# A graph network's second feed-forward matmul split into three float32r terms, with the splitting shared among VectorE and GpSimd

## What is computed

```python
# layer 0
attn_out = attn_out @ Wo + bo
h1 = _layer_norm(x + attn_out, g1, be1)
ff = jax.nn.relu(h1 @ W1 + b1) @ W2 + b2        # W1 512x1024, W2 1024x512
return _layer_norm(h1 + ff, g2, be2)
...
# layer 1
edge_feat = jnp.concatenate([x[src], x[dst], edge_attr], axis=-1)
h = mish(edge_feat @ W1 + b1)
messages = mish(h @ W2 + b2)
agg = jax.ops.segment_sum(messages, dst, num_segments=x.shape[0])
...
x = _layernorm(x + _L0_gnn_ref(...), axis=-1)
x = _layernorm(x + _L1_gnn_ref(...), axis=-1)
```

## Time and profile before

| | before |
|---|---|
| median of three runs | 244.72 us |
| the profiled execution | 245.73 us |
| its span, first to last instruction | 243.8 us |
| PE busy | 230.8 us, 95% |
| DVE busy | 153.4 us, 63% |
| ACT busy | 120.6 us, 49% |
| POOL busy | 6.8 us, 3% |
| granted TensorE clock, mean | 0.990 |
| DMA moved | 25.48 MB |

### The profile page before, as it was taken

One profiled execution on the slowest core, in us unless ns is written; L12 is line 12 of the kernel. 1 busy time (PEld: TensorE's weight loads), 2 busy tenths in 40 slices (PEclk: granted clock), 3 DMA queues, 4 the chain that ended last, 5 costly groups with the idle time before them and its releaser, 6 DMA issues.

```text
span 243.8 us, 3226 instructions
## 1 busy us (share of the span) xinstructions
PE 230.8 (95%) x1231; PEld 185.9 (76%) x1231; DVE 153.4 (63%) x271; ACT 120.6 (49%) x220; POOL 6.8 (3%) x18
## 2 busy tenths in 40 slices
PE   7999999998999999999999999999999999997980
PEld 3977788765676787888888888888888889996760
DVE  3639785577579655875856848758558454363625
ACT  0326198747729834745735646457355343244000
POOL 0020000001000000000000000000000000000001
PEclk9999999999999999999999999999999999999995
DMA  6999979930690000009022050040000000000001
GB/s 208 307 400 386 397 249 383 356 137 0 163 255 15 0 0 0 3 8 330 5 100 76 0 172 1 9 166 0 0 0 3 0 0 0 3 0 0 3 0 44
DMA packets 12320, 25.48 MB, mean 105 GB/s; under 512 B 1017, under 2 KB 1937, under 8 KB 11921
## 3 DMA queue, kind: packets, MB, share of 16 engines
q1 hardware_dynamic: 11520, 24.78, 30.0%
q10 hardware_dynamic: 784, 0.50, 0.8%
HBM read 25.01 MB, written 0.26 MB: 104 GB/s over the span
## 4 chain that ended last, share of the span: by engine, by line
PE 86%; DVE 6%; ACT 3%; issue 2%; POOL 1%; POOLq 0%; DVEq 0%; ACTq 0%
PE bank L668 36%; PE bank L651 12%; PE bank L463 9%; PE bank L472 6%; PE bank L519 4%; PE bank L535 3%; PE bank L678 3%; PE bank L679 3%; PE bank L482 2%; PE bank L446 1%; ACT WsT L408 1%; PE bank L630 1%; DVE y L884 1%; PE bank L631 1%; PE bank L635 1%
## 5 line engine op out<-in xcount | busy, mean ns | idle before, releaser
L668 PE MATMUL bank<-W2hi,Hhi 128*128 128x512 f32 x128 | 49.8, 389 | 0.0
L668 PE MATMUL bank<-W2hi,Clo 128*128 128x512 f32 x128 | 49.8, 389 | 0.0
L668 PE MATMUL bank<-W2lo,Hhi 128*128 128x512 f32 x128 | 49.8, 389 | 0.0
L380 ACT ACTIVATE Mhi<-M 128x512 fp32r<-128x512 f32 x32 | 20.2, 632 | 45.4 <-DVE M L994 45.4
L999 DVE TENSOR_TENSOR Mlo<-M,Mhi 128x512 fp32r<-128x512 f32 x32 | 22.1, 690 | 24.4 <-ACT M L381 24.4
L994 DVE TENSOR_TENSOR M<-bank,b2r 128x512 f32<-128x512 f32 x32 | 22.0, 687 | 12.6 <-PE bank L679 7.6
L668 PEld LDWEIGHTS bank<-W2hi,Clo 128*128 128x128 f32 x128 | 24.0, 188 | 5.0
L668 PEld LDWEIGHTS bank<-W2hi,Hhi 128*128 128x128 f32 x128 | 24.0, 188 | 5.0
L668 PEld LDWEIGHTS bank<-W2lo,Hhi 128*128 128x128 f32 x128 | 24.0, 188 | 5.0
L373 ACT ACTIVATE Hhi<-C 128x512 fp32r<-128x512 f32 x32 | 20.0, 625 | 12.4 <-DVE C L980 12.1
L293 ACT ACTIVATE C<-bank,cols 128x512 f32<-128x512 f32 x32 | 19.9, 685 | 11.6 <-PE bank L519 11.5
(11 more groups left out here) (193 smaller groups left out, 314.6 us busy)
## 6 DMA issues: line engine op xcount, KB each, us to landing
F<-in_L_gnn_W SPq DMA_DIRECT2D x2, 2048.0 KB, 14.3
W1raw<-in_L_gnn_W SPq DMA_DIRECT2D x1, 2048.0 KB, 22.5
ids<-in_src SPq DMA_DIRECT2D x2, 1024.0 KB, 14.0
W<-in_L_gnn_W SPq DMA_DIRECT2D x1, 2048.0 KB, 8.6
Wq<-in_L_gnn_Wq SPq DMA_DIRECT2D x4, 256.0 KB, 4.5
Wk<-in_L_gnn_Wk SPq DMA_DIRECT2D x4, 256.0 KB, 7.0
Wv<-in_L_gnn_Wv SPq DMA_DIRECT2D x1, 1024.0 KB, 10.1
ea<-in_edge_attr SPq DMA_DIRECT2D x1, 1024.0 KB, 11.8
```

The costliest lines, as they stand in the source:

```text
L380: act.activation(Mhi[:, t, :], M[:, t, :], ACT.Mish)
L668: done = mm(ST2[t][:, :], x[:, c, e], w[:, c, :], start=c == 0 and i == 0, stop=c == KC - 1 and i == 2)
```

## The change

It makes the second feed-forward of three float32r terms. ffT is rounded to `ffThi` by DVE and its remainder `ffTlo` made by POOL; F2 is rounded to `F2hi` by DVE, in the place of F1: the chunk pair i goes to the columns that group i of the first feed-forward has used, so it waits for `f1_done`. POOL makes `F2lo`. PE then does 48 float32r matmuls instead of 16 float32 ones, with the same edge steps between. F2 is loaded in W1raw's place of the queue and the reverse; W2raw's place is now used by ffThi, and its load waits for `f2_done` = 2. ACT makes W1hi behind the relus, among its edge steps. W1's remainders are shared: chunks 0 to 3 by POOL behind the feed-forward's, 4 and 5 by DVE behind the one-hots, 6 and 7 by DVE around the casts of xs.

```diff
-                        ("F2", 24, 8, F32), ("MA", 48, 4, F32), ("W2raw", 52, 4, F32), ("attn", 56, 2, F32), ("Wo", 60, 4, F32),
-                        ("W1raw", 64, 8, F32), ("EAThi", 72, 4, F32R), ("Wchi", 76, 1, F32R), ("Wc", 77, 1, F32), ("ffT", 78, 2, F32),
+                        ("W1raw", 24, 8, F32), ("MA", 48, 4, F32), ("W2raw", 52, 4, F32), ("attn", 56, 2, F32), ("Wo", 60, 4, F32),
+                        ("F2", 64, 8, F32), ("EAThi", 72, 4, F32R), ("Wchi", 76, 1, F32R), ("Wc", 77, 1, F32), ("ffT", 78, 2, F32),
...
+        split = overlay(("F2hi", 16, 8, F32R), ("W1lo", 24, 8, F32R), ("ffThi", 52, 2, F32R), ("xhi", 78, 1, F32R), ("xlo", 79, 1, F32R))
...
+        F2hi = split["F2hi"].rearrange("p (a h i n) -> p i a h n", a=2, h=2, i=FC // 2)
...
-            sp.dma_start(W1raw, w_view(a["L1_gnn_W1"][0:2 * D, :])).then_inc(S["w1_in"], 16)
+            sp.dma_start(F2, w_view(a["L0_gnn_W2"])).then_inc(S["f2_in"], 16)
...
-            sp.dma_start(F2, w_view(a["L0_gnn_W2"])).then_inc(S["f2_in"], 16)
+            sp.dma_start(W1raw, w_view(a["L1_gnn_W1"][0:2 * D, :])).then_inc(S["w1_in"], 16)
...
+            sp.wait_ge(S["f2_done"], 2)
             sp.dma_start(W2raw, w_view(a["L1_gnn_W2"])).then_inc(S["w2_in"], 16)
...
+            inverse_deviation(1)
+
+            for i in range(FC // 2):
+                for k in (2 * i, 2 * i + 1):
+                    pool.wait_ge(S["f2_hi"], k + 1)
+                    pool.tensor_tensor(F2lo[:, k, :].rearrange("p (h n) -> p h n", h=2), F2[:, k, :].rearrange("p (h n) -> p h n", h=2),
+                                       F2hi[:, i, k % 2].bitcast(F32), ALU.subtract).then_inc(S["f2_lo"], 1)
+                pool.wait_ge(S["ff_hi"], i + 1)
+                two = slice(2 * i, 2 * i + 2)
+                pool.tensor_tensor(ffTlo[:, two, :], ffT[:, two, :], ffThi[:, two, :].bitcast(F32), ALU.subtract).then_inc(S["ff_lo"], 1)
+            for c in range(KC):
+                pool.wait_ge(S["w1_hi"], c // 2 + 1)
+                pool.tensor_tensor(W1lo[:, c, :], W1raw[:, c, :], W1hi[:, c, :].bitcast(F32), ALU.subtract).then_inc(S["w1_lo_dst"], 1)
+            for n in range(1, 8):
+                inverse_deviation(n + 1)
...
-            act.wait_ge(S["w1_in"], 16)
             for i in range(4):
-                w1_high(i)
                 relu_out(i)
                 if i >= 1:
                     edge_term_out(range(i - 1, i))
             features_high(3)
-            edge_term_out(range(3, RING_STEPS))
+            act.wait_ge(S["w1_in"], 16)
+            for i in range(4):
+                w1_high(i)
+                edge_term_out(range(i + 3, i + 4))
+            edge_term_out(range(7, RING_STEPS))
...
-                columns_by((bank[1], bank[2]), ffT, F2, h, range(0, 3), 0, FC - 1)
+            def second_feed_forward(h, ks):
+
+                for k in ks:
+                    pe.wait_ge(S["f2_hi"], k + 1)
+                    pe.wait_ge(S["ff_hi"], k // 2 + 1)
+                    part = slice(D // 2 * h, D // 2 * (h + 1))
+                    whole = (bank[1], bank[2])[h][:, 0:D // 2]
+                    mm(whole, ffThi[:, k, :], F2hi[:, k // 2, k % 2, h, :], start=k == 0, stop=False)
+                    pe.wait_ge(S["f2_lo"], k + 1)
+                    mm(whole, ffThi[:, k, :], F2lo[:, k, part], start=False, stop=False)
+                    pe.wait_ge(S["ff_lo"], k // 2 + 1)
+                    done = mm(whole, ffTlo[:, k, :], F2hi[:, k // 2, k % 2, h, :], start=False, stop=k == FC - 1)
+                return done
...
-            for c in range(2 * KC):
-                dve.wait_ge(S["w1_hi"], c // 2 + 1)
-                v.tensor_tensor(W1lo[:, c, :], W1raw[:, c, :], W1hi[:, c, :].bitcast(F32), ALU.subtract).then_inc(S["w1_lo"], 1)
+            dve.wait_ge(S["f2_in"], 16)
+            for i in range(FC // 2):
+                dve.wait_ge(S["f1_done"], i + 1)
+                for k in (2 * i, 2 * i + 1):
+                    v.tensor_copy(F2hi[:, i, k % 2], F2[:, k, :].rearrange("p (h n) -> p h n", h=2)).then_inc(S["f2_hi"], 1)
+                dve.wait_ge(S["ff_ready"], 2 * (i + 1))
+                two = slice(2 * i, 2 * i + 2)
+                v.tensor_copy(ffThi[:, two, :], ffT[:, two, :]).then_inc(S["ff_hi"], 1)
...
             source_onehots(1)
+            w1_low((4, 5))
...
             norm(y[:, :], xs[:, :], S["nx_ready"])
+            w1_low((6,))
...
+            w1_low((7,))
             out_halves(xT_flat, xs_banks, S["nT_done"], 2, S["nT_ready"])
```

More of the change, by code:

```diff
@@ L96, in gnn_kernel @@
         first = overlay(("Wq", 0, 4, F32), ("Wk", 4, 4, F32), ("Wv", 8, 4, F32), ("ea", 12, 4, F32), ("F1", 16, 8, F32),
-                        ("F2", 24, 8, F32), ("MA", 48, 4, F32), ("W2raw", 52, 4, F32), ("attn", 56, 2, F32), ("Wo", 60, 4, F32),
-                        ("W1raw", 64, 8, F32), ("EAThi", 72, 4, F32R), ("Wchi", 76, 1, F32R), ("Wc", 77, 1, F32), ("ffT", 78, 2, F32),
+                        ("W1raw", 24, 8, F32), ("MA", 48, 4, F32), ("W2raw", 52, 4, F32), ("attn", 56, 2, F32), ("Wo", 60, 4, F32),
+                        ("F2", 64, 8, F32), ("EAThi", 72, 4, F32R), ("Wchi", 76, 1, F32R), ("Wc", 77, 1, F32), ("ffT", 78, 2, F32),
                         ("rows", 80, 7, F32), ("EATlo", 91, 4, F32R))
-        other = overlay(("Dbf", 28, 4, BF16), ("Sbf", 52, 4, BF16), ("W1hi", 56, 8, F32R), ("W1lo", 64, 8, F32R),
-                        ("ids0", 48, 4, I32), ("ids1", 87, 4, I32), ("Wclo", 77, 1, F32R), ("xhi", 78, 1, F32R), ("xlo", 79, 1, F32R))
+        other = overlay(("Dbf", 28, 4, BF16), ("Sbf", 52, 4, BF16), ("W1hi", 56, 8, F32R), ("F2lo", 64, 8, F32R), ("ffTlo", 78, 2, F32R),
+                        ("ids0", 48, 4, I32), ("ids1", 87, 4, I32), ("Wclo", 77, 1, F32R))
+        split = overlay(("F2hi", 16, 8, F32R), ("W1lo", 24, 8, F32R), ("ffThi", 52, 2, F32R), ("xhi", 78, 1, F32R), ("xlo", 79, 1, F32R))
         low = overlay(("Clo", 0, 32, F32R), ("Mlo", 64, 4, F32R))
@@ L119, in gnn_kernel @@
         Dbf, Sbf = chunks(other["Dbf"], ET), chunks(other["Sbf"], ET)
-        W1hi, W1lo = chunks(other["W1hi"], 2 * KC), chunks(other["W1lo"], 2 * KC)
-        xhi, xlo = chunks(other["xhi"], KC), chunks(other["xlo"], KC)
+        W1hi, W1lo = chunks(other["W1hi"], 2 * KC), chunks(split["W1lo"], 2 * KC)
+        xhi, xlo = chunks(split["xhi"], KC), chunks(split["xlo"], KC)
+        ffThi, ffTlo, F2lo = chunks(split["ffThi"], FC), chunks(other["ffTlo"], FC), chunks(other["F2lo"], FC)
+        F2hi = split["F2hi"].rearrange("p (a h i n) -> p i a h n", a=2, h=2, i=FC // 2)
         C = edge["C"].rearrange("p (g j e) -> p g j e", g=G, j=KC)
@@ L276, in _, with inverse_deviation @@
             inverse_root(1, small[:, 1:2], small[:, 2:3], S["deg_ready"], S["dinv_ready"])
-            for n in range(8):
-                inverse_root(n + 1, mv[:, 1:2], rstd[:, :], S["stat_ready"], S["rstd_ready"])
+            def inverse_deviation(n):
+                inverse_root(n, mv[:, 1:2], rstd[:, :], S["stat_ready"], S["rstd_ready"])
+            inverse_deviation(1)
[12 more added lines that the diff above has]
+                inverse_deviation(n + 1)
         @block.scalar
@@ L605, in _ @@
             turn_features(3)
-            pe.wait_ge(S["f2_in"], 16)
+            def second_feed_forward(h, ks):
[10 more added lines that the diff above has]
+                return done
             for h in range(2):
-                columns_by((bank[1], bank[2]), ffT, F2, h, range(0, 3), 0, FC - 1)
+                second_feed_forward(h, range(0, 3))
                 edge_term(range(2 * h + 3, 2 * h + 4))
-                columns_by((bank[1], bank[2]), ffT, F2, h, range(3, FC - 2), 0, FC - 1)
+                second_feed_forward(h, range(3, 6))
                 edge_term(range(2 * h + 4, 2 * h + 5))
-                if h == 0:
-                    pe.wait_ge(S["ff_ready"], FC)
-                columns_by((bank[1], bank[2]), ffT, F2, h, range(FC - 2, FC), 0, FC - 1).then_inc(S["f2_done"], 1)
+                second_feed_forward(h, range(6, FC)).then_inc(S["f2_done"], 1)
                 if h == 0:
@@ L624, in _ @@
             pe.wait_ge(S["w1_hi"], 4)
-            pe.wait_ge(S["w1_lo"], 8)
+            pe.wait_ge(S["w1_lo_dst"], KC)
             for b, c0 in ((bank[1], 0), (bank[2], KC)):
@@ L636, in _ @@
                 done.then_inc(S["ab_done"], 1)
+                if c0 == 0:
+                    pe.wait_ge(S["w1_lo"], KC)
             pe.wait_ge(S["nT_ready"], 4)
@@ L928, in _, with w1_low @@
             features_low(2)
-            for c in range(2 * KC):
-                dve.wait_ge(S["w1_hi"], c // 2 + 1)
-                v.tensor_tensor(W1lo[:, c, :], W1raw[:, c, :], W1hi[:, c, :].bitcast(F32), ALU.subtract).then_inc(S["w1_lo"], 1)
+            dve.wait_ge(S["f2_in"], 16)
[6 more added lines that the diff above has]
+                v.tensor_copy(ffThi[:, two, :], ffT[:, two, :]).then_inc(S["ff_hi"], 1)
             features_low(3)
+            def w1_low(cs):
```

(3 more changed lines are left out.)

4 lines of the change are left out of this document (2 added, 2 removed).

## The result

| us | before | after |
|---|---|---|
| time, median | 245.2 (244.4 to 246.1, 4 runs) | 253.4 (253.2 to 253.8, 4 runs) |
| span of the profiled execution | 243.8 | 251.7 |
| its mean granted clock of PE | 0.990 | 0.975 |

The change makes the kernel slower by 3.4%, a ratio of 1.034 [1.032, 1.036], or 8.2 us. The prediction had the sign and too little of the size: 2.3 us, with 249.8 as its upper end.

What follows compares the result with a forecast made beforehand. It took the chain as PE's up to 56.69, then DVE's normalisation. Terms +1.1, +1.2, +1.2 and -0.55 made +3.0, or +1.6 with shorter POOL slots; the middle, +2.3, gave 248.0 from 245.73, median 247.0, range 244.8 to 249.8.

Steps and rivals of the forecast that it cites:

- PE's matmuls: Second feed-forward on PE: 48 float32r matmuls at 0.12 us replace 16 float32 ones, saving 1.3 us in all.
- POOL, right in the sum: POOL's feed-forward subtractions: 1.26 us each, 0.70 for half size, plus 1.5 for casts between; last piece at 51.2.
- The casts, held: DVE's casts from SBUF between POOL's subtractions: 0.15 us each, between 0 and 0.3; ten make 1.5 us.
- The prediction's sum by the pages, 249.2: Whole kernel if DVE and POOL block one another in full, a cast at 0.3 us: 249.2 us.
- DVE starts the graph copies at 52.2: DVE behind PE's graph transposes: copies start at 52.2 where they were at 51.09, +1.1 us.
- The step that failed: DVE's one-hots beside POOL: taken as single rate, 0.66 to 0.71 us for 512 elements, and not held.
- The first is held until 56.2: +1.2: First of DVE's two new W1 subtractions, behind the one-hots: held by POOL's W1 subtractions until 56.2, +1.2 us.
- The new subtractions +1.2 and the residual -0.55: DVE before the statistics: two W1 subtractions at 0.60 us add 1.2; the residual no longer waits for PE, -0.55.
- What was costed at nothing: W1lo(6) ahead of xhi's casts, W1lo(7) and xT, ACT's W1hi, W2hi's later load, exchanged F2 and W1raw loads: no cost.
- Rival 3, the clock: PE's clock falls in a 3 us pause before the transposes of xs: 2.3 to 3.5 us more, 249.9; chance 0.12.
- Rivals 1 and 2: DVE beside POOL: first, nothing held, 244.9 us, chance 0.22; second, only two-input instructions held, 245.6 us, chance 0.14.
- the prediction's upper one: Delay at DVE's statistics with POOL's slot at 1.26 us: +3.0, against +1.6 with a slot of 1.17.

Runs made afterwards that it cites:

- forms kernel: Separate kernel computing nothing of the reference: eight VectorE instruction forms, alone, then beside five GpSimd subtractions 128x512; a cast went from 0.45 to 1.16 us.
- 16 rounds of filler: Changed kernel plus 16 idle bf16 matmuls of 512 columns on PE before the transposes of xs: 252.7 us, ratio 1.030.
- 26 rounds of filler: Changed kernel plus 26 rounds of idle matmuls on PE between edge steps 9 and 10 and the transposes of xs: 251.8 us, ratio 1.026.

## Why the prediction was right and wrong

- **PE's matmuls, right.** The saving was there: 0.83 us at the graph copies and 0.55 at the residual in the run without the hold and without the two W1lo, where 1.3 in all was forecast. The transposes' release needed POOL, as forecast; the pitch of a float32r matmul of 256 columns was the 0.12 taken (55.87, 55.98, 56.10 in PE's order of time after) while the clock was whole.
- **POOL, right in the sum, by luck.** Its last feed-forward piece ended at 51.11; forecast 51.2. The errors of the parts cancel: a slot of 1.35 with its cast, not 1.26 + 0.15 or 1.17 + 0.15, but a start at 36.61, and 0.91 for the half size (1.10 for the last), the upper bound and not the 0.70 taken.
- **The casts, held, as L884 had suggested.** 1.2 us each beside POOL against 0.42 without it. By the Trainium skill (page "SBUF — State Buffer", section "Who interferes with whom") the engine that comes second to the shared ports is blocked in full. The forms kernel agrees that each holds the other: 0.45 to 1.16 us, and POOL's 1.23 to 1.37. What a cast adds to POOL is (6.84 - 6.15)/4 = 0.17 us, near the 0.15 taken and not the 0.3 of "in full". The prediction's sum by the pages, 249.2, was short too, for it left the one-hots out like the other. (The word cast stands in that section; the section "Mode 2×_2P" that the prediction names for it speaks of `tensor_scalar` and `tensor_copy`.)
- **"DVE starts the graph copies at 52.2", wrong.** PE's transposes did stand at 51.96 and 52.17. DVE came at 54.73, since it was still at its one-hots.
- **The step that failed: "The one-hots L938 take 0.66 to 0.71 us for 512 elements, the single rate; I take them as not held."** They were held: +2.94 and +1.70 us where the sum had nothing. Undoing POOL's W1 brought 2.0 and 1.66 of that back, adding it to the kernel before made 2.44 into 5.50, and the forms kernel shows it alone. 0.68 us was no evidence: the same comparison on contiguous integers takes 0.51, so the strided form is slowed by its pattern and is still of the kind that POOL holds. The Trainium skill, page "VectorE: DVE Perf Modes", section "What auto-detection actually checks", asks, for the mode that uses both ports, for a single source and a destination in SBUF whose outermost dimensions are both even or equal, and names no stride for it: by it the one-hots, which are `tensor_scalar`, are such instructions, and the runs agree (0.68 to 1.63 us beside GpSimd). I had cited the mode for the casts and not applied it to the instruction beside them.
- **"The first is held until 56.2: +1.2", wrong in place.** The two W1lo of DVE were not held (1.28 for both), because POOL had ended at 57.64 while the one-hots in front of them had been. The hold lies on what DVE runs from SBUF beside POOL's 6.56 us.
- **The new subtractions +1.2 and the residual -0.55: both right**, at 1.20 and 0.55.
- **What was costed at nothing stayed so**: L979's third and fourth, ACT's W1hi, W2hi (no wait on W2raw), the exchanged loads.
- **Rival 3, the clock**, was given 0.12 and came true on top of the hold: forecast 2.3 to 3.5 us after a pause of 3 us; measured 4.65 us of pause, and 1.9 (chain) to 2.4 (filler) us. It was wrong to keep it as a case apart: every forecast that has DVE late by 2 us has the pause too, and in this kernel pauses of 1.96 and 2.0 us were enough in most runs.
- **Rivals 1 and 2** fell with the holding of casts and one-hots. The argument for rival 1, that POOL's 0.55 us instruction had not held a two-input L855, was weak: that instruction has one element a row. (Its end of POOL at 49.2 is also not the 49.7 of the prediction's own sum; nothing rests on it.)

The sum with what was measured, from the prediction's upper one (+3.0, 2.95 before rounding): 2.95 - 1.2 (W1lo not held) + 1.70 (second one-hots) + 2.54 (graph copies at +3.64, not +1.1) = 6.0 at the mark, and 1.9 to 2.4 for the clock, 7.9 to 8.4 against 8.2. The clock also stood at 0.68 from 50 to 54 in after, behind PE's 1.59 us wait on POOL. PE was not on the chain there, and it cost nothing at the mark: the profiled run with 16 rounds of filler had 1.00 there and the mark at 63.83, against 63.74. What stays open is which executions keep the clock after such a pause.

## What to carry to other kernels

GpSimd's share of the busy time says nothing of what it costs: before work goes there, list every VectorE instruction that will run beside it, and count those that read only SBUF at GpSimd's duration, whatever rate they show alone. If VectorE is on the chain, a tensor that nobody needs yet is better made in a stretch where VectorE reads PSUM or waits; that is argued from the forms above, and no run moved POOL's subtractions there. Work moved onto the chain to make room for a saving has to be set against it: here 1.2 us of subtractions stood against 1.3 us of quicker matmuls. And a delay on one engine is a pause on TensorE: price the clock with the delay, not as a case by itself.

## What the runs showed of the hardware

- A VectorE instruction with all tensor inputs in SBUF was held beside a GpSimd subtraction in every form tried (1.03 to 1.63 us for 0.32 to 0.71 alone), one with an input in PSUM in none of two.
- The holding goes both ways: GpSimd's subtraction took 1.23 us beside PSUM forms, 1.37 beside casts, 1.60 beside two SBUF inputs. In the changed kernel its slot was 1.35 beside casts and 1.64 beside one-hots.
- The granted clock fell to its lower level after pauses of 1.96, 2.0 and 2.49 us that stood behind edge steps with gaps of their own, and after one of 2.56 behind 3.6 us of filler, in most executions and not in all: about 3.3 us between the two groups of one kernel's runs, 244.9 to 245.1 and 248.1 to 248.7. Filling the pause made all twelve executions alike.
- A pause of 1.59 to 1.60 us, the wait for POOL ahead of the graph transposes, stands alike in four profiles: the clock fell to 0.50 behind it in two (after, and 26 rounds of filler) and stayed at 1.00 in two (no W1 on POOL, and 16 rounds).
